# A depthwise convolution in an expert layer: from channel layout on VectorE to token layout on GpSimd

## The reference, cut to what matters

```python
# hidden_states: [1, 512, 512] (tokens, channels), after a layer norm; KC = 4
g = jnp.einsum('th,ehi->tei', x, Wg); u = jnp.einsum('th,ehi->tei', x, Wu)
mlp_out = jnp.einsum('tei,eih->teh', jax.nn.silu(g) * u, Wd)
routed = jnp.einsum('te,teh->th', cw[:, :E_MLP], mlp_out)
routed = routed + (cw[:, 4:5] + cw[:, 6:7]) * x + cw[:, 7:8] * jax.nn.relu(x)
shared = lax.conv_general_dilated(hidden_states, conv_w, (1,), padding=[(KC - 1, 0)],
             dimension_numbers=('NHC', 'HIO', 'NHC'), feature_group_count=512) + conv_b
return routed + shared            # added to the residual
```

## Time and profile before

| | |
|---|---|
| median of three runs | 538.21 us |
| the profiled execution, whole | 538.51 us |
| its span, first to last instruction | 536.7 us |
| PE busy | 528.3 us, 98% |
| DVE busy | 360.8 us, 67% |
| ACT busy | 249.7 us, 47% |
| POOL busy | 198.6 us, 37% |
| DMA traffic | 51.58 MB |

### The profile page before, as it was taken

One profiled execution on the slowest core, in us unless ns is written; L12 is line 12 of the kernel. 1 busy time (PEld: TensorE's weight loads), 2 busy tenths in 40 slices (PEclk: granted clock), 3 DMA queues, 4 the chain that ended last, 5 costly groups with the idle time before them and its releaser, 6 DMA issues.

```text
span 536.7 us, 6796 instructions
## 1 busy us (share of the span) xinstructions
PE 528.3 (98%) x2450; PEld 439.2 (82%) x2450; DVE 360.8 (67%) x618; ACT 249.7 (47%) x415; POOL 198.6 (37%) x134
## 2 busy tenths in 40 slices
PE   8899999999999999999999999999999999999997
PEld 7788788888888888888888888888888888888886
DVE  5474656876567866566878554999966517538757
ACT  5652343755544544454545354557365452551210
POOL 2629041321311222234144432547359929800000
PEclk9999999999999999999999999999999999999999
DMA  8801323242332224422322221243421304200002
GB/s 286 324 22 56 119 79 110 88 156 79 102 134 78 78 85 151 149 87 79 133 103 79 80 74 45 78 158 117 151 85 34 124 2 152 84 1 0 1 1 78
DMA packets 15152, 51.58 MB, mean 96 GB/s; under 512 B 1808, under 2 KB 2320, under 8 KB 14480
## 3 DMA queue, kind: packets, MB, share of 16 engines
q1 hardware_dynamic: 15120, 51.16, 26.9%
HBM read 50.11 MB, written 1.05 MB: 95 GB/s over the span
## 4 chain that ended last, share of the span: by engine, by line
PE 95%; DVE 2%; DMA 1%; SPq 1%; ACT 1%; issue 0%
PE bank L1372 27%; PE bank L1479 11%; PE bank L1480 11%; PE bank L1478 11%; PE bank L1467 11%; PE bank L1469 10%; PE bank L1468 10%; PE bank L1362 1%; DMA wv_raw<-wv_in 1%; PE bank L1592 1%; PE bank L1601 1%; DVE ct_l L958 0%; DVE xT_l L909 0%; PE bank L1720 0%; PE bank L1554 0%
## 5 line engine op out<-in xcount | busy, mean ns | idle before, releaser
L554 POOL TENSOR_TENSOR cn_l<-raw_n,cn_h 128x1024 fp32r<-128x1024 f32 x32 | 77.7, 2428 | 197.3 <-ACT cn_h L713 197.3
L731 ACT COPY ring<-bank 128x512 f32<-128x512 f32 x64 | 37.7, 589 | 149.7 <-PE bank L1469 149.4
L1467 PE MATMUL bank<-qk_h,ct_h 128*128 128x512 f32 x256 | 99.7, 389 | 1.1 <-DVE top L1028 1.1
L1028 DVE TENSOR_TENSOR top<-top,bank 128x512 f32<-128x512 f32 x60 | 41.2, 686 | 87.4 <-ACT ring L731 86.9
L1469 PE MATMUL bank<-qk_h,ct_l 128*128 128x512 f32 x256 | 99.6, 389 | 0.0
L1468 PE MATMUL bank<-qk_l,ct_h 128*128 128x512 f32 x256 | 99.6, 389 | 0.0
L1478 PE MATMUL bank<-ph,cn_h 128*128 128x512 f32 x256 | 99.6, 389 | 0.0
L1479 PE MATMUL bank<-pl,cn_h 128*128 128x512 f32 x256 | 99.6, 389 | 0.0
L1480 PE MATMUL bank<-ph,cn_l 128*128 128x512 f32 x256 | 99.6, 389 | 0.0
L1467 PEld LDWEIGHTS bank<-qk_h,ct_h 128*128 128x128 f32 x256 | 48.1, 188 | 11.5 <-DVE ct_l L958 1.5
L1468 PEld LDWEIGHTS bank<-qk_l,ct_h 128*128 128x128 f32 x256 | 48.1, 188 | 10.0
(11 more groups left out here) (237 smaller groups left out, 868.3 us busy)
## 6 DMA issues: line engine op xcount, KB each, us to landing
raw_t<-ctx_t SPq DMA_DIRECT2D x32, 512.0 KB, 4.2
raw_n<-ctx_n SPq DMA_DIRECT2D x32, 512.0 KB, 3.3
piece_raw<-pieces SPq DMA_DIRECT2D x12, 512.0 KB, 3.3
xs<-x SPq DMA_DIRECT2D x4, 256.0 KB, 5.2
wq_raw<-wq_t SPq DMA_DIRECT2D x4, 256.0 KB, 6.3
wk_raw<-wk_in SPq DMA_DIRECT2D x1, 1024.0 KB, 7.7
w_k_raw<-wqkv_in SPq DMA_DIRECT2D x1, 1024.0 KB, 7.3
w_out_raw<-wout_in SPq DMA_DIRECT2D x1, 1024.0 KB, 5.4
```

The costliest lines, as they stand in the source:

```text
L554: pool.tensor_tensor(cn[p % CNB][1][:], raw_n[p % 2][:], cn[p % CNB][0][:].bitcast(F32), ALU.subtract).then_inc(cnl_ready, 1)
L1028: dve.tensor_tensor(top[:], top[:], bank[:, S_BANKS[i % 2], :], ALU.max).then_inc(max_done, 1)
L1467: pe.matmul(bank[:, dst, :], ct[i // 2 % 2][0][:, c, keys], qk[0][:, c, :], start=(c == 0), stop=False)
```

## The change

The convolution is computed in token layout, on POOL. Its four taps and its bias come once as five rows, spread over all partitions (taps, 128 x 2560 values, 1.31 MB written). That load stands on SP behind the issue of piece 8.

A token shifted by j places lies in another partition, so SP issues transfers inside SBUF: for each tile and each j = 1, 2, 3 the rows 0 to 127 - j of xn go to rows j to 127 of shifted, and, for tiles 1 to 3, the last j rows of the tile before go to its first j rows. The rows ahead of token 0 are set to zero by POOL. There are two buffers. The first is filled for tile 0 as soon as the pieces have been issued, the second for tile 1 once gates(1) is done (it lies where piece 0 was), and tiles 2 and 3 wait until the convolution of tile 0 and of tile 1 is complete.

POOL multiplies xn by the tap of no shift, adds the bias, and for each j multiplies and adds: 8 instructions of 128 x 512 for a tile, 32 in all, each waiting for the one ahead. DVE adds the four results to xs in step m = 6. The whole copies on ACT, the taps on DVE and the 16 transposes on PE are gone, and with them the waits on them. On DVE add_expert(2) now stands ahead of the last low_hid.

```diff
@@ SP
                 sp.wait_ge(piece_ready, n - 1)
                 sp.dma_start(piece_raw[n % 2][:], pieces[n]).then_inc(piece_loaded[n % 2], 16)
+                if n == 8:
+                    sp.wait_ge(kv_psum, C)
+                    sp.dma_start(taps[:], taps_in.partition_broadcast(P)).then_inc(taps_loaded, 16)
+
+            sp.wait_ge(la_psum, TT)
+            sp.wait_ge(pads_ready, 2)
+            for t in range(TT):
+                b = t % 2
+                sp.wait_ge(xn_ready, 2 * TT + t + 1)
+                if t == 1:
+                    sp.wait_ge(g_psum, IC)
+                if t >= 2:
+                    sp.wait_ge(conv_ready, t - 1)
+                for j in range(1, TAPS):
+                    sp.dma_start(shifted[b][j:P, j - 1, :], xn[0:P - j, t, :]).then_inc(shift_loaded[b], 16)
+                    if t > 0:
+                        sp.dma_start(shifted[b][0:j, j - 1, :], xn[P - j:P, t - 1, :]).then_inc(shift_loaded[b], 16)
@@ POOL
-            pool.memset(xf[:, :, 0:PAD], 0.0).then_inc(pads_ready, 1)
+            pool.memset(shifted[0][0:PAD, :, :], 0.0).then_inc(pads_ready, 1)
...
+            pool.wait_ge(taps_loaded, 16)
+            for t in range(TT):
+                pool.wait_ge(xn_ready, 2 * TT + t + 1)
+                conv_chain(pool.tensor_tensor(conv[:, t, :], xn[:, t, :], taps[:, PAD, :], ALU.mult))
+                conv_chain(pool.tensor_tensor(conv[:, t, :], conv[:, t, :], taps[:, TAPS, :], ALU.add))
+                pool.wait_ge(shift_loaded[t % 2], 16 * (2 * PAD * (t // 2 + 1) - PAD * (1 - t % 2)))
+                for j in range(1, TAPS):
+                    conv_chain(pool.tensor_tensor(tap_term[:], shifted[t % 2][:, j - 1, :], taps[:, PAD - j, :], ALU.mult))
+                    ins = pool.tensor_tensor(conv[:, t, :], conv[:, t, :], tap_term[:], ALU.add)
+                    if j < PAD:
+                        conv_chain(ins)
+                ins.then_inc(conv_ready, 1)
@@ ACT
-            for t in range(TT):
-                whole_xT(t)
@@ DVE
-            dve.wait_ge(pads_ready, 2)
-            dve.wait_ge(xf_ready, TT)
             for m in range(M):
...
-                if 2 <= m < 2 + C:
-                    c = m - 2
-                    conv_chain(dve.tensor_scalar(conv[:, c, :], xf[:, c, 0:T], tap(0), col("conv_b", c), ALU.mult, ALU.add))
-                    for j in range(1, TAPS):
-                        ins = dve.scalar_tensor_tensor(out=conv[:, c, :], in0=xf[:, c, j:j + T], scalar=tap(j),
-                                                       in1=conv[:, c, :], op0=ALU.mult, op1=ALU.add)
...
+                if m == M - 2:
+                    for t in range(TT):
+                        dve.wait_ge(conv_ready, t + 1)
+                        add_term(t, conv[:, t, :], None)
+            add_expert(EM - 2)
             low_hid(M - 1)
-            add_expert(EM - 2)
-            for t in range(TT):
-                dve.wait_ge(conv_psum, t + 1)
-                add_term(t, bank[:, t, :], None)
@@ PE
-            pe.wait_ge(conv_ready, C)
-            pe.wait_ge(silu_ready, M)
-            pe.wait_ge(hid_full_ready, M)
-            for t in range(TT):
-                for c in range(C):
-                    ins = pe.transpose(bank[:, t, c * P:(c + 1) * P], conv[:, c, t * P:(t + 1) * P], ident[:])
-                ins.then_inc(conv_psum, 1)
             down(M - 2)
             down(M - 1)
```

More of the change, by code:

```diff
@@ L63 @@
 NCOLS = 0
-for _name, _n in (("bq", C), ("bk", C), ("bv", C), ("qn", C), ("conv_b", C), ("conv_w", C * TAPS), ("wr", C * E)):
+for _name, _n in (("bq", C), ("bk", C), ("bv", C), ("qn", C), ("wr", C * E)):
     COLS[_name] = NCOLS
@@ L69, with perceiver_block @@
 NROWS = 3 * D + E
-def perceiver_block(nc, x, ctx_t, ctx_n, wq_t, wk_in, wv_in, wo_t, wqkv_in, wout_in, pieces, cols_in, rows_in, out):
+def perceiver_block(nc, x, ctx_t, ctx_n, wq_t, wk_in, wv_in, wo_t, wqkv_in, wout_in, pieces, cols_in, rows_in, taps_in, out):
     with ExitStack() as stack:
@@ L214, in perceiver_block @@
         order = {(kind, e): n for n, (kind, e) in enumerate(PIECES)}
-        xf = at(160, "xf", [P, C, PAD + T])
+        shifted = [at((160, 128)[b], f"shifted{b}", [P, PAD, D]) for b in range(2)]
+        taps = at(84, "taps", [P, TAPS + 1, D])
+        tap_term = at(94, "tap_term", [P, D])
         score_rows = at(168.25, "score_rows", [2 * E, T])
@@ L218, in perceiver_block @@
         tied = at(171.25, "tied", [P, TT, E, E])
-        conv = at(48, "conv", [P, C, T])
+        conv = at(48, "conv", [P, TT, D])
         relu_x = at(56, "relu_x", [P, 2, D])
@@ L260, in perceiver_block @@
         run_cleared = sem("run_cleared")
-        bv_term_ready = sem("bv_term_ready")
         bv_psum = sem("bv_psum")
@@ L285, in perceiver_block @@
         xl_ready = sem("xl_ready")
-        xf_ready = sem("xf_ready")
         q_psum = sem("q_psum")
@@ L362, in perceiver_block @@
         down_psum = sem("down_psum")
-        conv_psum = sem("conv_psum")
+        taps_loaded = sem("taps_loaded")
+        shift_loaded = [sem(f"shift_loaded{b}") for b in range(2)]
         out_ready = sem("out_ready")
@@ L600, in _, with conv_chain @@
                 split_piece(n)
+            steps = [0]
+            def conv_chain(ins):
+                ins.then_inc(conv_step, 1)
+                steps[0] += 1
+                pool.wait_ge(conv_step, steps[0])
+            pool.wait_ge(taps_loaded, 16)
[10 more added lines that the diff above has]
+                ins.then_inc(conv_ready, 1)
         def terms_with(e, t):
-            return e * TT + t + 1 + 2 * min(TT, IC * (e + 1))
+            return e * TT + t + 1 + 2 * min(TT, IC * (e + 1)) + (TT if e == EM - 2 else 0)
         XT_BANKS = (0, 1, 2, 3)
@@ L826, in _ @@
                 high_xT(3 * TT + t, HEAD_BANKS)
[L829 to L833, removed]
             std_of(2 * TT)
@@ L1330, in _ @@
                     add_term(t, relu_x[:, t % 2, :], None)
-                if 2 <= m < 2 + C:
-                    c = m - 2
-                    def tap(j):
-                        return cols[:, COLS["conv_w"] + c * TAPS + j:COLS["conv_w"] + c * TAPS + j + 1]
-                    conv_chain(dve.tensor_scalar(conv[:, c, :], xf[:, c, 0:T], tap(0), col("conv_b", c), ALU.mult, ALU.add))
-                    for j in range(1, TAPS):
-                        ins = dve.scalar_tensor_tensor(out=conv[:, c, :], in0=xf[:, c, j:j + T], scalar=tap(j),
-                                                       in1=conv[:, c, :], op0=ALU.mult, op1=ALU.add)
-                        if j < TAPS - 1:
-                            conv_chain(ins)
-                    ins.then_inc(conv_ready, 1)
+                if m == M - 2:
[3 more added lines that the diff above has]
+            add_expert(EM - 2)
             low_hid(M - 1)
-            add_expert(EM - 2)
-            for t in range(TT):
-                dve.wait_ge(conv_psum, t + 1)
-                add_term(t, bank[:, t, :], None)
             for t in range(TT):
@@ L1633, in route @@
             def route():
-                pe.wait_ge(xf_ready, 1)
                 pe.wait_ge(xl_ready, 5 * TT)
@@ L1677, in down @@
                 if m == 0:
-                    pe.wait_ge(xf_ready, TT)
                     pe.wait_ge(route_step, 2)
@@ L1706, in _ @@
                     pe.wait_ge(rows_ready, 1)
-                    pe.wait_ge(xf_ready, 2)
                     for t in range(TT):
@@ L1759 @@
             [column(L0_xattn_bq), column(L0_xattn_bk), column(L0_xattn_bv), column(L0_attn_qn_w),
-             column(L0_ffn_conv_b),
-             np.asarray(L0_ffn_conv_w).reshape(TAPS, C, P).transpose(2, 1, 0).reshape(P, C * TAPS),
              on_partitions(L0_ffn_Wr).reshape(P, C * E)], axis=1)),
@@ L1764 @@
                                    (L0_xattn_bo, L0_attn_kn_w, L0_attn_b_out, L0_ffn_router_bias)]),
+        "taps_in": np.concatenate([np.asarray(v).reshape(-1) for v in (L0_ffn_conv_w, L0_ffn_conv_b)]),
     }
```

## The result

The changed kernel takes 544.92 us in the median of four runs (543.4 to 546.31), against 538.09 for the kernel before (the three runs told of above, and one more): a ratio of 1.0112, with a 95% interval of 1.0094 to 1.013. The forecast was slower, 548.6 us, within 541.5 to 554. The profiled execution took 545.45 us with a span of 543.4.

What follows compares the result with a forecast made beforehand. PE was taken to bound the kernel. POOL's late end put down(6) at 536.3, plus 5.47 and 0.75: 8.4 us later; with 2 for the clock, 10.4 on 538.51, so 548.6 us as median, range 541.5 to 554.

Steps and rivals of the forecast that it cites:

- What bounds: PE, busy 98% of the span, alone carries the end; of the convolution only its 16 transposes, 1.75 us, are on the path.
- The queue on DVE: Behind the convolution's last add stand experts(7), hid_l(6) and add_expert(2): four DVE instructions, 2.7 us, before down(6) can start.
- X: The end of POOL's last convolution instruction, forecast at 533.6 us.
- The limit of 523.5: PE is not delayed ahead of down(6) while POOL's last instruction ends before 523.5 us; each us after costs one.
- One engine for 127 rows: Shift transfers of 127 rows go on one DMA engine at 88 ns a row: 650 rows, 57.2 us, 466.8 to 524.0.
- POOL's chain: POOL's 32 chained sums and products start 1.39 us apart, 44.5 us; the six after tile 3's rows take 8.3 us.
- Collisions: DVE instructions with two SBUF inputs wait up to 1.3 us for POOL's running instruction and hold POOL up about 0.5.
- about the slack: Only the router's last five two-input DVE instructions meet POOL, costing about the 5 us hid_l(1) has before down(1).
- the starved router: Rival, chance 0.22: transfers spread wide, POOL runs without pause and slows DVE's router, PE waits at down(1): 542 to 552 us.
- The clock: PE's clock falls after its wait, so the last 24 matmuls take 0 to 5.5 us longer; 2 taken.
- The signs: First shift transfer over 11 us, tiles 14 us apart, POOL waiting for DMA, PE's longest wait ahead of down(6), slow two-input DVE instructions.
- The transfers' share of X: The string of shifted rows on one DMA engine sets when POOL can finish: it ends at 524.0 us.

Runs made afterwards that it cites:

- e3: Changed kernel with every shift transfer cut in two and POOL's 32 sums and products replaced by memsets, convolution left out: 536.29 us, ratio to the kernel before 0.9943.
- e5: Changed kernel with shift transfers cut, last tile's add behind the last low_hid, POOL waiting for the router's weights ahead of tile 1: 536.48 us, ratio to before 0.995.
- e6: Changed kernel with shift transfers cut and POOL waiting for the router's weights ahead of tile 1, all four adds in step 6: 536.36 us, ratio to before 0.9952.
- e9: Changed kernel with only the 127-row transfer cut, in 112 and 15 rows: 544.24 us, ratio to the kernel before 1.0095.
- e1: Changed kernel with every shift transfer cut in 112 rows and the rest: 543.55 us, ratio to the kernel before 1.008.
- e7: Changed kernel, transfers uncut, with POOL waiting for the router's weights ahead of tile 0's shifted taps: 547.63 us, ratio to the kernel before 1.0165.
- e2: Changed kernel, transfers uncut, with the last tile's add moved on DVE behind the last low_hid: 541.41 us, ratio to the kernel before 1.0044.
- e8: Changed kernel, transfers uncut, POOL waiting for the router's weights ahead of tile 0's shifted taps, tile 3's add right ahead of its last term: 538.77 us, ratio to before 1.0002.

## Why the prediction was right, and where its sizes were off

- **What bounds.** PE alone carries the end, and only the transposes are worth anything: right. e3, e5 and e6 show it in reverse: with nothing late they gain 0.5 to 0.6%; in e5 DVE ends 2.18 us sooner, the 1.75 us and 0.4 more.
- **The queue on DVE.** X is where the wait starts, with 2.7 us from it to down(6): POOL's end at 530.08 and down(6) at 532.82 give 2.74. The limit of 523.5 held in e6, which ended 0.6 us below it with no wait.
- **One engine for 127 rows.** Right, shown by the floor of 25 GB/s at the busy share of one engine, and by e9. The size was off: 85 ns a row and not 88, and the string began at 465.8 (479.45 less 161 rows) and not 466.8. The load of the taps was slower than I had put it, 7.2 us to land and not 6, but it delayed the rest less: SP issued piece 11 at 461.97 instead of 460.6, and POOL's last piece ended at 468.87, no later than the 469.19 of before. The last rows came at 520.8 instead of 524.0. That is 3.2 us of the 3.6 by which the end of POOL was forecast too late (530.1 against 533.6).
- **POOL's chain.** The products and sums came as closely as I had put them: the first two, above, start 1.38 us apart (468.83 and 470.21), against 1.39. The six last ones with their collisions took 9.2 us, against 9.6. In e1, where POOL waited for no rows, all 32 with their collisions took 47.1 us (470.05 to 517.15), against 44.5 without any.
- **Collisions.** The mechanism and the 1.3 us of a wait: right, and e3 shows that reads are the cause. What I put wrong is the place. I let tile 0's rows land at 481.3 (my own 161 rows of 88 ns from 466.8 make it 481.0), past nearly all of the comparisons, and called the damage "about the slack", though five waits of up to 1.3 us are up to 6.5, against 5 of slack. They landed 1.9 us sooner, the router met POOL on nearly its whole length, and PE waited 2.8 us. This was the rival's mechanism (the starved router) inside my own case. e1 is that rival built: 543.55 us, near the lower end of its 542 to 552. Eight comparisons cost neither 8 waits nor 1, but 4: two passed for each POOL instruction.
- **It added nothing to the end.** e7 shows why a second wait could be there without moving the sum: DMA and POOL, not PE, set the time of down(6). Without PE's 2.8 us at down(1) PE would have waited longer at down(6). That the sum came out near the measured time although it left this wait out was luck: had the transfers been shared out, as in e1, the same slow router would have cost 5.4 us and the clock behind it.
- **The clock.** I took 2 us out of 0 to 5.5 for the 24 matmuls behind the wait; it was 7.34 - 5.47 = 1.87.

- **The signs.** The tiles came 13.7 to 14.0 us apart, and POOL waited for DMA ahead of its third instruction of every tile: both as forecast. The third, that PE's longest wait stands ahead of down(6), failed: it is the 2.8 us ahead of down(1), against 2.5. No view shows when the first transfer landed by itself.

The sum of the forecast, 10.4 us on the profiled execution, stands against 6.9. Two steps failed. The transfers' share of X was wrong in size alone, and makes 3.2 us of the 3.5 too many. The overlap of the router with POOL was put at nothing and cost PE 2.8 us, which the later wait for the last tile covered.

## What to carry to other kernels

Work moved to an idle engine has two due times, that of its result and that of everything queued behind the instruction that takes it; a late add cost 4 us in the middle of DVE's queue and nothing at its end, as long as PE's last results came later still (e2). In e8, where they came sooner, the late add used up what the transposes gave. Before a transfer of 127 rows, look at how the number can be shared out: with 112 + 15 rows in its place (e9) POOL waited for no rows at all, and 125 and 126 rows needed no cut. And a chain on GpSimd that reads SBUF should not run beside a chain of small two-input instructions on VectorE: with the transfers cut, one wait for a semaphore ahead of tile 1 turned a ratio of 1.008 (e1) into 0.9952 (e6).

## What the runs showed of the hardware that was not expected

- **SP is held by the string.** Issues on SP in the changed kernel, of tile 1's edge row (start us, us) and of the twelve large transfers (ns min/median/max):

```profile
473.50 7.60 SPq L471 DMA_DIRECT2D shifted<-xn  x1
L469 SPq DMA_DIRECT2D shifted<-xn x12: 617/757/4462, 462.4 to 510.1; - x12
```

  What stands right behind a transfer of 127 rows was long in issue: the edge row of tile 1 took 7.60 us, those of tiles 2 and 3 took 6.41 and 4.77, and the 126 rows of tile 0 took 4.46. A part of a cut transfer in e1 took 0.5 to 0.9. In e9, where only the 127 rows are cut, no transfer inside SBUF took more than 1.74 to issue. Whether the issue of something else behind it, such as a store, would be held too was not seen.
- **A single-input instruction beside memsets.** In e3 the tensor_scalar of 128 x 4 took 1.11 us instead of 0.17 while POOL only wrote, and the two-input instructions around it took their usual time. In e1, beside POOL's products and sums, it took 1.07. So POOL's writes hold this one, and its reads the others, is the reading; it was not tested further. (The same section of the Trainium skill (SBUF — State Buffer, "Who interferes with whom") names tensor_scalar among the operations that can take both of VectorE's ports, and these contend with GpSimd; the 1.11 us agree, and no view shows whether this one did take both.)
- **The clock fell after short waits.** After 2.8 us of waiting at down(1) the granted clock was 0.83 over ten us, after 5.4 us 0.66, after 2.5 us ahead of down(6) 0.82 and 0.84. The longest wait of the kernel before, 1.4 us, left it at full in every slice. These are means over a stretch in which the clock was at 2.4 GHz for a part and at 1.2 for the rest.
